# A fused two-layer kernel on one core: retention rows read from their PSUM bank, the experts' bias and Gelu by ScalarE in four pieces, and a new order on every engine

## The reference, cut to what matters

```
layer 0:  xn = layernorm(x);  s = attention(xn);  g = silu(sigmoid(xr Wr) * (relu(xk Wk)^2 Wv));  x = x + s*g
layer 1:  xn = layernorm(x)
  retention, 16 heads of key 8, value 16:
    scores = (q k^T) * decay mask;  den = clip(sum|scores|, 1, 50000)
    ret = (scores/den) v;  ret = ret * rsqrt(mean(ret^2) + eps)
    s = ((x Wg + bg) * ret) Wo + bo
  soft mixture of 8 experts with 64 slots each:
    logits = xn . slots;  dispatch = softmax over rows;  combine = softmax over slots
    h = gelu(slots_e w1_e + b1_e);  eo = h w2_e + b2_e;  out = combine eo
  x = x + s * silu(out)
```

## Time and profile before

| what | us |
|---|---|
| median of 3 runs | 1120.39 |
| lowest and highest | 1118.67, 1120.84 |
| the profiled execution's own time | 1119.9 |
| its span, first to last instruction | 1118.0 |
| PE busy | 1075.3 (96%) |
| DVE busy | 931.1 (83%) |
| ACT busy | 800.5 (72%) |
| POOL busy | 604.6 (54%) |

### The profile page before, as it was taken

How to read it: one execution, slowest core, us unless ns; L and a number is a source line. 1 busy time by engine, 2 the same in 40 slices (tenths; PEclk the granted TensorE clock), 3 DMA queues, 4 the chain that set the end, 5 groups by cost and what they waited for, 6 DMA issues and landing times.

```text
span 1118.0 us, 28039 instructions
## 1 busy us (share of the span) xinstructions
PE 1075.3 (96%) x10436; PEld 831.2 (74%) x10436; DVE 931.1 (83%) x2074; ACT 800.5 (72%) x1481; POOL 604.6 (54%) x651
## 2 busy tenths in 40 slices
PE   5799999999999999999999999999999999999996
PEld 3468687777868778687777868778687777868775
DVE  3778889888897988889888897988889888897975
ACT  3386877868768686877868768686877868768674
POOL 3354647554574654647554574654647554574544
PEclk9899999999999999999999999999999999999999
DMA  6000000000000000000000000000000000000000
GB/s 252 10 2 11 1 11 12 10 12 1 21 1 11 11 11 12 1 11 11 11 11 1 20 2 11 11 11 11 2 11 11 11 11 1 20 2 11 1 11 11
DMA packets 18468, 16.97 MB, mean 15 GB/s; under 512 B 800, under 2 KB 17440, under 8 KB 18080
## 3 DMA queue, kind: packets, MB, share of 16 engines
q1 hardware_dynamic: 18336, 15.18, 4.1%
HBM read 10.98 MB, written 4.19 MB: 14 GB/s over the span
## 4 chain that ended last, share of the span: by engine, by line
PE 74%; DVE 16%; issue 7%; ACT 2%; POOL 1%; POOLq 0%; DMA 0%; DVEq 0%; SPq 0%; ACTq 0%
PE bank L971 10%; PE bank L961 10%; PE bank L1010 8%; PE bank L981 5%; PE bank L952 5%; PE bank_s L992 5%; PE bank L922 4%; PE bank L825 3%; DVE ret L670 3%; PE bank L856 3%; PE bank L910 3%; PE bank L1020 3%; PE bank L876 3%; DVE mx L714 2%; DVE xn L558 2%
## 5 line engine op out<-in xcount | busy, mean ns | idle before, releaser
L344 POOL TENSOR_TENSOR urs<-uvar,mhalf 128x16 f32<-128x16 f32 x64 | 192.2, 3004 | 141.2 <-DVE uvar L686 141.2
L339 POOL TENSOR_TENSOR ret_abs<-ret_abs 128x512 f32<-128x512 f32 x128 | 163.5, 1277 | 175.3 <-ACT ret_abs L484 173.1
L670 DVE TENSOR_TENSOR ret<-bank_s,k_sb 128x1536 f32<-128x1536 f32 x128 | 223.6, 1747 | 24.5 <-PE bank L1010 22.4
L484 ACT ACTIVATE ret_abs<-ret 128x1536 f32<-128x1536 f32 x128 | 189.5, 1481 | 34.0 <-DVE ret L670 30.7
L971 PEld LDWEIGHTS bank<-w_sb,hact 128*128 128x128 f32 x1024 | 121.6, 192 | 28.6 <-issue 16.1
L971 PE MATMUL bank<-w_sb,hact 128*128 128x128 f32 x1024 | 132.4, 280 | 1.4 <-ACT hact L479 1.4
L961 PEld LDWEIGHTS bank<-slotsT,w_sb 128*128 128x128 f32 x1024 | 120.6, 192 | 12.1 <-issue 11.3
L961 PE MATMUL bank<-slotsT,w_sb 128*128 128x128 f32 x1024 | 125.7, 276 | 0.2 <-ACT slotsT L474 0.2
L1010 PE MATMUL bank<-ret,vrow 128*32 128x256 f32 (+1 forms) x2048 | 109.1, 330 | 0.6 <-POOL ret_abs L339 0.6
L735 DVE TENSOR_TENSOR hact<-bank,v_sb 128x512 f32<-128x512 f32 x128 | 88.2, 689 | 17.3 <-PE bank L961 11.9
L479 ACT ACTIVATE hact<-hact 128x512 f32<-128x512 f32 x128 | 76.8, 623 | 32.5 <-DVE hact L735 32.1
(11 more groups left out here) (143 smaller groups left out, 2432.9 us busy)
## 6 DMA issues: line engine op xcount, KB each, us to landing
x_sb<-x SPq DMA_DIRECT2D x16, 256.0 KB, 2.7
w_sb<-w SPq DMA_DIRECT2D x2, 2048.0 KB, 14.0
out<-attn SPq DMA_DIRECT2D x16, 256.0 KB, 2.3
v_sb<-vectors SPq DMA_DIRECT2D x1, 832.0 KB, 7.4
w_sb<-weights SPq DMA_DIRECT2D x1, 512.0 KB, 4.9
k_sb<-consts SPq DMA_DIRECT2D x1, 466.0 KB, 5.9
w_sb<-weights SPq DMA_DIRECT2D x1, 320.0 KB, 3.2
slot_sb<-slot_rows SPq DMA_DIRECT2D x1, 256.0 KB, 3.3
```

Of the source, the lines that this page charges most:

```text
L339: pool.tensor_tensor(both[:, :, P:SEQ], both[:, :, P:SEQ], both[:, :, SEQ:3 * P], ALU.add)\
L344: pool.tensor_tensor(urs[:, j], uvar[:, j], mhalf[:], ALU.pow).then_inc(ready["urs"].sem, 1)
L484: act.activation(ret_abs[:, q % MR], ret[:, q % MR], ACT.Abs).then_inc(ready["ab"].sem, 1)
L670: dve.tensor_tensor(ret[:, q % MR], bank_s[:, :, 0:3 * P], causal.unsqueeze(1).broadcast_to([P, Q, 3 * P]), ALU.mult)\
```

## The change

What it does:

- `U` goes. `usq` squares straight from the bank of `row`, and `rowd` reads the denominators and values from the bank too. `rowd` now waits for `usq`, and the bank is free when `rowd` has made `ug` (in `READ_BY`: `"row": "ug"`).
- `hb` goes. `hg` waits for the bank of `h` and for `eo` e-2, and applies Gelu with the bias in four instructions of 128x128, each with its own bias column. The bank is free when the fourth is done (`"h": "hg"`).
- `sgT` moves from POOL to ACT, as two 128x256 instructions with a bias column.
- A one-column Exp (`warm`) runs on ACT before the early loads are waited for. `derived` comes after the first `stat` on DVE, and POOL waits for it after the first `rstd`.
- All four lists of `ORDER` and the table `BANK` are new. `eo` 6, `eo` 7, `row` 2, `row` 3, both `out`, `cs` 3, `ce` 3 and `eoc` 3 are age 2 now and `xn2T` is age 1; `gatedT` 0 is age 1.

```
             def hg(p, par, e):
-                act.wait_ge(*ready["hb"](p, e))
-                act.activation(hact[:, e % 2], hact[:, e % 2], ACT.Gelu).then_inc(ready["hg"].sem, 1)
+                bank = bank_of("h", p, e)
+                since(act, filled["eo"], *((p, e - 2) if e >= 2 else (p - 1, e - 2 + E)))
+                for c in range(HC):
+                    ins = act.activation(hact[:, e % 2, c], bank[:, c * P:(c + 1) * P], ACT.Gelu,
+                                         bias=V["b1"][:, e * HC + c:e * HC + c + 1])
+                ins.then_inc(ready["hg"].sem, 1)
...
-            def U_(p, par, j):
+            def usq_(p, par, j):
                 bank = bank_of("row", p, j)
                 since(act, ready["uvar"], *((p, j - 2) if j >= 2 else (p - 1, j + 2)))
-                act.activation(U[:, j % 2], bank[:].rearrange("p (h v) -> p h v", h=HEADS), ACT.Copy)\
-                    .then_inc(ready["U"].sem, 1)
-
-            def usq_(p, par, j):
-                act.wait_ge(*ready["U"](p, j))
-                act.activation(usq[:, j % 2], U[:, j % 2, :, 0:VD], ACT.Square).then_inc(ready["usq"].sem, 1)
+                act.activation(usq[:, j % 2], bank[:].rearrange("p (h v) -> p h v", h=HEADS)[:, :, 0:VD], ACT.Square).then_inc(ready["usq"].sem, 1)
...
             def rowd(p, par, j):
-                dve.wait_ge(*ready["U"](p, j))
-                dve.tensor_scalar(den[:, j], U[:, i, :, VD], 1.0, 50000.0, ALU.max, ALU.min).then_inc(ready["den"].sem, 1)
-                dve.tensor_tensor(ug[:, j], U[:, i, :, 0:VD], grow[:, j], ALU.mult)
+                u = banks[BANK["row", j]][:].rearrange("p (h v) -> p h v", h=HEADS)
+                dve.wait_ge(*ready["usq"](p, j))
+                dve.tensor_scalar(den[:, j], u[:, :, VD], 1.0, 50000.0, ALU.max, ALU.min).then_inc(ready["den"].sem, 1)
+                dve.tensor_tensor(ug[:, j], u[:, :, 0:VD], grow[:, j], ALU.mult).then_inc(ready["ug"].sem, 1)
...
+            act.wait_ge(ready["setup"].sem, 4)
+            act.activation(warm[:], mhalf[:, 0:1], ACT.Exp)
             act.wait_ge(early.sem, 48)
```

More of the change, by code:

```diff
@@ L75 @@
[L75 to L78, removed]
[9 rows of a table removed]
-             ("urs", 0, 1), ("sgT", 0, 0), ("add", 5, 1), ("add", 6, 1), ("urs", 1, 1), ("add", 7, 1),
-             ("rstd2", 0, 0), ("rnorm", 0, 0)],
-}
@@ L93 @@
-BANK = {("DT", 0): 0, ("DT", 1): 3, ("DT", 2): 2, ("DT", 3): 2, ("LT", 0): 3, ("LT", 1): 1, ("LT", 2): 2,
[4 rows of a table removed]
-        ("local", 0): 0, ("mxT", 0): 2, ("o", 0): 1, ("o", 1): 2, ("out", 0): 1, ("out", 1): 2, ("qk", 0): 0,
-        ("qk", 1): 3, ("r", 0): 2, ("rB", 0): 0, ("row", 0): 1, ("row", 1): 3, ("row", 2): 2, ("row", 3): 3,
-        ("s", 0): 3, ("score", 0): 1, ("score", 1): 0, ("slots", 0): 2, ("slots", 1): 1, ("srow", 0): 0,
-        ("v", 0): 2, ("vg", 0): 0, ("vg", 1): 1, ("vg", 2): 3, ("vg", 3): 2, ("xn2T", 0): 0, ("xn3T", 0): 2,
-        ("xnT", 0): 1}
[5 rows of a table added]
+           ("slots", 0, 1), ("slots", 1, 1), ("mxT", 0, 1), ("g", 2, 1), ("g", 3, 1), ("quad", 4, 1),
[5 rows of a table added]
@@ new lines @@
+    "ACT": [("ce", 3, 2), ("usq", 2, 2), ("usq", 3, 2), ("xn2Tc", 0, 1), ("zt", 0, 2), ("xn3Tc", 0, 1),
+            ("LTc", 0, 1), ("LTc", 1, 1), ("DTe", 0, 1), ("LTc", 2, 1), ("xnTc", 0, 0), ("DTe", 1, 1),
+            ("LTc", 3, 1), ("ab", 0, 1), ("sT", 0, 0), ("Dc", 0, 1), ("DTe", 2, 1), ("Dc", 1, 1), ("DTe", 3, 1),
+            ("gTc", 1, 2), ("ab", 1, 1), ("eTc", 0, 0), ("Dc", 2, 1), ("RTc", 0, 1), ("Dc", 3, 1), ("ab", 2, 1),
+            ("RTc", 1, 1), ("ab", 3, 1), ("sgT", 0, 0), ("slc", 0, 1), ("slc", 1, 1), ("RTc", 2, 1), ("RTc", 3, 1),
[4 rows of a table added]
+            ("RTc", 6, 1), ("ce", 2, 1), ("RTc", 7, 1)],
@@ new lines @@
+    "POOL": [("rnorm", 0, 1), ("rstd", 0, 0), ("urs", 2, 2), ("urs", 3, 2), ("km", 0, 1), ("dn", 0, 1),
+             ("km", 1, 1), ("dn", 1, 1), ("add", 0, 1), ("km", 2, 1), ("dn", 2, 1), ("mixa", 0, 0), ("dn", 3, 1),
+             ("km", 3, 1), ("add", 1, 1), ("km", 4, 1), ("add", 2, 1), ("add", 3, 1), ("km", 5, 1), ("km", 6, 1),
+             ("add", 4, 1), ("urs", 0, 1), ("add", 5, 1), ("km", 7, 1), ("urs", 1, 1), ("add", 6, 1), ("add", 7, 1),
+             ("rstd2", 0, 0)],
+}
+BANK = {("DT", 0): 2, ("DT", 1): 3, ("DT", 2): 2, ("DT", 3): 0, ("LT", 0): 0, ("LT", 1): 1, ("LT", 2): 3,
[4 rows of a table added]
+        ("local", 0): 2, ("mxT", 0): 0, ("o", 0): 2, ("o", 1): 3, ("out", 0): 2, ("out", 1): 3, ("qk", 0): 0,
+        ("qk", 1): 3, ("r", 0): 3, ("rB", 0): 1, ("row", 0): 1, ("row", 1): 2, ("row", 2): 1, ("row", 3): 0,
+        ("s", 0): 3, ("score", 0): 3, ("score", 1): 0, ("slots", 0): 3, ("slots", 1): 2, ("srow", 0): 0,
+        ("v", 0): 1, ("vg", 0): 1, ("vg", 1): 0, ("vg", 2): 2, ("vg", 3): 1, ("xn2T", 0): 3, ("xn3T", 0): 1,
+        ("xnT", 0): 2}
@@ L103 @@
 READ_BY = {"xnT": ("xnTc", 0), "s": ("sT", 0), "global": ("gbias", 0), "e": ("eTc", 0), "srow": ("srowc", 0),
            "score": "P", "PT": "PTc", "local": ("field", 0), "r": ("tr", 0), "k": ("kr", 0), "v": ("rv", 0),
-           "xn2T": ("xn2Tc", 0), "xn3T": ("xn3Tc", 0), "qk": "qkc", "vg": "vgc", "LT": "LTc", "mxT": ("rmax", 0), "rB": ("rBc", 0), "DT": "Dc", "slots": "slc", "h": "hb", "eo": "eoc", "row": "U", "g": "RTc", "gatedT": "gTc", "o": "attn",
+           "xn2T": ("xn2Tc", 0), "xn3T": ("xn3Tc", 0), "qk": "qkc", "vg": "vgc", "LT": "LTc", "mxT": ("rmax", 0), "rB": ("rBc", 0), "DT": "Dc", "slots": "slc", "h": "hg", "eo": "eoc", "row": "ug", "g": "RTc", "gatedT": "gTc", "o": "attn",
@@ L300, in mixa @@
                 ins.then_inc(ready["mixa"].sem, 1)
-            def sgT_(p, par, k):
-                pool.wait_ge(*ready["gbias"](p))
-                since(pool, filled["srow"], p - 1)
-                pool.sem_inc(passed["gpsimd"].sem, 1)
-                for b in range(2):
-                    ins = pool.tensor_scalar(sgT[:, b], sT[:, b], gbias[:, b:b + 1], 0.0, ALU.add, ALU.add)
-                ins.then_inc(ready["sgT"].sem, 1)
             def rstd2_(p, par, k):
@@ L383, in sT_ @@
                 since(act, filled["score"], p - 1, 1)
-                since(act, ready["sgT"], p - 1)
                 for b in range(2):
@@ L388, in sT_, with sgT_ @@
                 ins.then_inc(ready["sT"].sem, 1)
+            def sgT_(p, par, k):
+                act.wait_ge(*ready["gbias"](p))
+                since(act, filled["srow"], p - 1)
+                for b in range(2):
+                    ins = act.activation(sgT[:, b], sT[:, b], ACT.Identity, bias=gbias[:, b:b + 1])
+                ins.then_inc(ready["sgT"].sem, 1)
             def eTc(p, par, k):
@@ L793, in _ @@
                            "stat2": stat2_, "xn2": xn2_, "xn3": xn3_, "qkc": qkc, "vgc": vgc, "ret": ret_, "rowd": rowd,
-                           "gated": gated_, "attn": attn_, "LTm": LTm, "mx": mx_, "rmax": rmax_, "cs": cs, "drec": drec_, "hb": hb, "eoc": eoc,
+                           "gated": gated_, "attn": attn_, "LTm": LTm, "mx": mx_, "rmax": rmax_, "cs": cs, "drec": drec_, "eoc": eoc,
                            "z": z_, "zg": zg, "sg": sg, "x2": x2_}, ORDER["DVE"],
-                     between={("smax", 1): slots_scaled, ("stat2", 0): slots_turned})
+                     between={("stat", 0): derived, ("smax", 1): slots_scaled, ("stat2", 0): slots_turned})
         @block.tensor
```

62 lines of the change are left out of this document (27 added, 35 removed), and 37 rows, old and new, of tables (BANK, ORDER).

## The result

The changed kernel takes 1109.24 us (median of 4 runs, 1109.1 to 1109.51), the kernel before 1119.62 in the same comparison: a ratio of 0.9907, 95% interval 0.989 to 0.9924. It is faster by 0.93%. The forecast was 1115, half of that gain; the time lies in the range and outside of the forecast's own 1111 to 1118.

What follows compares the result with a forecast made beforehand. PE was taken as the bound, 66.45 us busy of 67.08 a pair. With -2.0 over 15 pairs and -3.4 in the ramps, 1119.9 became 1114.5, so a median of 1115; range 1109 to 1128.

Steps and rivals of the forecast that it cites:

- Wait for `xn` gone, DVE near 52, POOL off the path: PE's 0.6 us wait per pair before `xnT` goes; DVE falls from 57.8 to some 52.3; POOL loses `sgT`.
- A piece is 0.26, an `hg` 1.04: On ACT, each 128-column Gelu from PSUM costs 0.26 us, bounds 0.16 and 0.36; four make an `hg` of 1.04.
- the slower rival: ACT's Gelu pieces cost more, 0.29 each, and PE waits for them: 1126 us, chance 0.33.
- PE's own work is 66.45 and "0.63 us of each pair are all that it stands still": PE busy 66.45 of 67.08 us a pair, taken as unchanged work; at most 0.63 a pair to win back.
- changes of kind: PE going from one kind of matmul to another in the new order: under 0.1 us a pair.
- First stretch waits 0.2, second 0.15: PE waits for ACT 0.2 us from `h` 0 to second `PT`, 0.15 from end of `local` to `h` 7.
- The walk: Summing PE and ACT tasks over two stretches: 14.0 against 14.2 us in the first, 5.9 against 6.05 in the second.
- Last pass: No term of its own; counted within the 15 pairs that together gain 2.0 us.
- Start -1.9, with +1.2 for `r`, `k` and `srow` ahead of the scores: First pair: `stat` earlier -1.8, table load of 1.28 us off the path, scores delayed 1.2 (between 0 and 3); sum -1.9.
- End -1.0: After the last `o`: -0.8 as the end waits only for `gTc` and eight instructions, -0.2 for `U`.
- PE waits for nothing: Rival: a Gelu piece below 0.24, a pair at 66.5 to 66.6, time 1109 us; chance 0.13.
- ACT's pieces put the wait where `xn` was: Rival: a larger Gelu piece makes PE wait in the same two stretches; 1126 us at 0.29; chance 0.33.

Runs made afterwards that it cites:

- before_one_mv: Kernel before with `hg` 4 moved ahead of `tr`, `hb` dropped, one 128x512 Gelu from PSUM per expert, bias left out: 1205.35 us, ratio 1.0768.
- hb_back: Kernel after, its order kept, with `hb` back on DVE, placed by hand, and one 128x512 Gelu from SBUF per expert: 1171.62 us, ratio 1.0467.
- early_second: Kernel after with a one-column Gelu added ahead of `sp`, so the second table load falls into ACT's idle time: 1099.28 us, ratio 0.9818.
- old_start: Kernel after with the start of before: no early table load, `derived` ahead of the first `stat`: 1111.42 us, ratio 0.9928.
- sgt_pool: Kernel after with `sgT` back on POOL as two 128x256 sums behind `add` 3: 1112.85 us, ratio 0.9939.

## Why the prediction had half of the gain

- *Wait for `xn` gone, DVE near 52, POOL off the path:* right (53.3). The reason given, both DVE's load and `xn`'s place, was half right: before_one_mv and hb_back show that the place did it.
- *A piece is 0.26, an `hg` 1.04:* right, 0.255 and 1.02. The Trainium skill's price ("ScalarE: Activation LUTs", section "What ACT_TABLE_LOAD costs"), 0.29 and 1.18, is not borne out by these rows, and the slower rival that it supported did not come. The measurement decides.
- *PE's own work is 66.45 and "0.63 us of each pair are all that it stands still":* **this step failed.** It read the busy column as work. By the starts, the kernel after, at 66.38 busy, still waits 0.46 at the second `PT` and 0.57 between `h` 5 and the second `eo`; early_second removed the latter and its busy time fell to 65.81. The kernel before hid waits in the same way:

```profile
396.57 0.66 PE L944 MATMUL bank<-k_sb,dT 128*128 128x128 f32 x4
397.80 0.66 PE L825 MATMUL bank<-k_sb,xn 128*128 128x128 f32 x4 [0.57 <-DVE xn L558]
```

  From the product ahead of the late `xnT` to `xnT` it is 1.23 where such a product takes 0.49, so the 0.6 of the earlier trace rows was 0.74. Its `eo` 6 and 7 hold PE for 2.10, where the kernel after has 1.89. The weight loads' rows of its waits view had 0.8 for `xn` and 0.7 for `hact` in this pair. Summed over one pair (the fifth of each trace), the holds of the product kinds of `DT`, `vg` and `eo` fell from 2.74, 3.90 and 7.85 to 1.80, 3.54 and 7.48, those of `PT` and `h` rose from 0.87 and 7.22 to 1.38 and 7.69, and all others together rose from 44.46 to 44.88, in small amounts where the kind of product changes. So a pair won 1.67 and lost 0.98 + 0.42, where the forecast had 0.63 won, 0.5 lost and under 0.1 for changes of kind: -0.27 instead of -0.13. What `vg` waited for was not taken apart. One more edit won 0.7. The Trainium skill says in "Perfetto Trace Analysis", section "Identifying the Most-Contended Engine", that the busy share of the matmul row is not a good measure of how close one is to the roofline, because pipelined instructions look smaller in the trace. This case's rows agree that it is no measure of headroom, but by the opposite error: the column was too large, by 0.57 us a pair.
- *First stretch waits 0.2, second 0.15:* measured 0.46 and 0.57. The walk had the lengths nearly right: from `h` 0 to the second `PT` 14.40 against 14.2 on ACT and 14.0 on PE. The second `PT` and `h` 7 were named rightly, from the order alone; the wait of `eo` 4 for `hg` 4, 0.3 of the 0.57, was not, and `srow`, also named, does not wait (`k` ahead of it holds PE for 0.86).
- *Last pass:* not reckoned at all beyond one more pair at -0.13; it brought -2.33. The kernel before waits there for the table load in front of an `hg`, too (PE's timeline, the last pass):

```profile
1090.13 0.61 PE L1010 MATMUL bank<-ret_abs,k_sb 128*32 128x256 f32 x8
1091.96 0.71 PE L971 MATMUL bank<-w_sb,hact 128*128 128x128 f32 x4 [1.21 <-ACT hact L479]
```

  That is 1.2 of the 2.33; the rest is spread over small distances and was not taken apart.
- *Start -1.9, with +1.2 for `r`, `k` and `srow` ahead of the scores:* measured -3.59 to the first `xn2T`. old_start puts 2.95 of it on `stat` and the table load, where the forecast had 3.1, so the order gave -0.64 and the sign of that term was wrong. The three keep PE at work while ACT and DVE prepare the scores:

```profile
15.05 2.05 PE L878 MATMUL bank<-w_sb,mix 128*128 128x128 f32 x8
16.89 1.15 PE L884 MATMUL bank<-mix,w_sb 128*128 128x512 f32 x2
18.04 0.65 PE L819 MATMUL bank<-k_sb,xn 128*128 128x128 f32 x4
18.61 2.06 PE L850 MATMUL bank<-sT,spin 128*128 128x256 f32 x8
```

  The scores end at 20.7 with the three done; before, they ended at 22.8 with the three still to come, and took 3.75 for the same eight instructions. By its durations the kernel before ran them at the lower clock, 1.2 GHz, as it did the product ahead of them, which takes half as long in a later pair:

```profile
16.24 2.06 PE L845 MATMUL bank<-sT,w_sb 128*128 128x512 f32 x2
...
411.21 1.02 PE L845 MATMUL bank<-sT,w_sb 128*128 128x512 f32 x2
```

  Its windows view reads 1.00 there, but the trace has no record of the clock ahead of 24.01, and the view prints 1.00 where there is none. In the kernel after the records begin at 17.15, with 1.00; `r` at 15.05 still takes 1.84 to the next start, in a later pair 0.98. sgt_pool shows what a gap does there: 3.3 idle, then a clock of 0.50 and 3.62 for the scores. `sgT` on ACT, which the forecast priced for ACT alone, is what makes this possible. `stat` at 3.67 and the table load at 0.71 are as forecast.
- *End -1.0:* -0.67; `gTc` at 1099.99 and one group of eight behind it (2.07) are as described.

Of the 5.3 us between the forecast (-5.4) and the traces (-10.7), the fourteen pairs make 2.0, the last pass 2.2 and the start with the first pass 1.4; the end takes 0.3 back.

Of the rivals, "PE waits for nothing" named the time, 1109, and not the cause: PE waits for about 1.0 a pair. "ACT's pieces put the wait where `xn` was" named the cause and not the price.
